# Second attention turns four heads behind its scores with seven buffers, and GpSimd waits for the normalisation before it splits weights

## The chip, the cores and the metric

The kernel runs on one core of one Trainium2 chip. The metric is the time of one execution in microseconds (us), measured on the device; runs of the same kernel give a median. One further execution was taken with the hardware profiler, and all rows below are from it.

## The reference, cut to what matters

Two layers of attention and feed-forward over 2048 tokens of width 256, float32, each of the four parts followed by a residual sum and a normalisation of the row:

```
x = layernorm(x + attention0(x))      # 16 heads, polynomial
x = layernorm(x + ffn0(x))            # dense, 1024 hidden
x = layernorm(x + attention1(x))      # 32 heads of 8 columns, softmax, in blocks of 256 tokens
x = layernorm(x + moe(x))             # shared expert + 2 of 8 experts

# attention1, for each of the 8 blocks of 256 tokens
scores = (q @ k.T) / sqrt(8) + rel_bias[None, None]
attn   = softmax(scores, axis=-1)
ctx    = attn @ v
out    = ctx @ wo.T
```

The change lies in attention1, in the loads and splits of the expert weights that run beside it, and in the first part of the mixture of experts, which uses those weights.

## The kernel before, in words

The program is written engine by engine: SyncE (SP) issues the loads and stores, TensorE (PE), ScalarE (ACT), VectorE (DVE) and GpSimd (POOL) each have one list of instructions, and semaphores hold them together. Every engine works its own list strictly in the order of the program. There are four phases: 0 and 1 (first attention and first feed-forward, interleaved), 2 (second attention, `phase2` on each engine), 3 (`moe`).

**Phase 2** makes eight iterations, one for each block of 256 tokens. In each, all engines step through the 32 heads with `for h in range(H2)`. The work of one head is a chain:

1. `scores` (PE): at every even h the scores of heads h and h+1, four matmuls, into one of three PSUM banks (`SCORE_BANKS`). It waits until `least` of head h-2 is done (`biased_ready`).
2. `least` (DVE): adds the bias, finds the row minimum of the negated scores, writes `prob(h)`, one of four SBUF buffers, and `mneg`. It waits for the scores, and until the turn of head h-4 has read the buffer.
3. `exponential` (ACT): exp of `prob(h)` in place, two instructions.
4. `turn` (PE): four transposes of `prob(h)` into one of two PSUM banks. At step h, head h-2 is turned. It waits for the exp of that head and until the head two before it has been taken out of its bank.
5. `take`: the turned head is copied to SBUF, by ACT for six heads of eight (`on_act`), by DVE for the other two. ACT takes head h-2 at its step h, ahead of exp(h); DVE takes head h-3 at its step h.
6. `mix` (PE): every fourth step, the product of four heads with V, sixteen matmuls.

Between these, at steps given by the tables `PE2`, `ACT2` and `DVE2`, lies all other work of the iteration: for the next block the transpose of x (`x_turn`), the projections (`qk`, `v`), their splits in a high and a low part (`hi_parts`, `lo_parts`), the transposes of the heads (`heads`, 8 transposes); for the block before, the division (`context`), its transposes (`c_turn`, `ct_turn`), the output projection (`project`), and on DVE the residual sum, the statistics (`add`) and the normalisation (`norm`). `x_turn` waits for the last copies of the heads (`heads_out`), because it uses the same bank.

**GpSimd in phase 2** splits weights of the mixture of experts in high and low parts: per iteration i the gate and up weights of expert i (`expert_part(i, 0)`), half a unit of the shared expert (`shared_part(i)`), and the down weights of expert i (`expert_part(i, 1)`, not in the last). `split` is one copy and one subtraction, both from the one raw buffer `wraw`; when it is done, SP may load the next piece (`raw_free`). After that GpSimd computes the reciprocal deviation for block i (`layernorm_rstd`), for which DVE's `norm` waits, and goes straight on to the split of the next expert.

**Phase 3** starts with 18 gate/up products of the shared expert on PE (`gate_up(n)`), with the router's choice on DVE between them (`choose`, `slots_in`). GpSimd first does constants, `layernorm_rstd` of the last block, and then the last three splits: the shared unit `SH_KEPT` (needed by `gate_up(4)`), half a unit (needed by `gate_up(5)`), and the down weights of expert 7. Then it scatters the tokens, for which it waits for `slots_ready`.

Of the kernel before, what the change touches and what calls it, by code (L numbers as in the profile page):

```python
# [30 lines left out]
P = 128  # L31
# [54 lines left out]
MIX_BANK = 4  # L86

# [4 lines left out]
def program(nc, x, rope, ln, aw0, wu1, aw2, rel, wu3, router, sel, out):  # L92
    with ExitStack() as ctx:
# [130 lines left out]
        mneg = small[:, 312:320]  # L224
# [159 lines left out]
        def dmas(load):  # L384

            e, kind = divmod(load - LOADS[2], 3)
            if load < LOADS[2]:
                return 1
            if load == LOADS3:
                return 4  # L390
            return 2 * len(list(pieces(e))) if kind == 0 and e < NEXP else 1
# [48 lines left out]
        def _(sp):  # L440
# [91 lines left out]
            def expert_weights(i):  # L532

                sp.wait_ge(raw_free, LOADS[2] + 3 * i + 1)
                for t, a, b, at in pieces(i):
# [4 lines left out]
                sp.wait_ge(raw_free, LOADS[2] + 3 * i + 2)  # L540
                half = slice(SH_HALF * (i % 2), SH_HALF * (i % 2 + 1))
                sp.dma_start(wraw[:, 0:SH_HALF], wu3[SH_FROM + i // 2, :, half]).then_inc(raw_ready, 16)
                if i == iterations[2] - 1:
                    return
# [27 lines left out]
            x3_rows(0, 4, rows_in)  # L572
            sp.wait_ge(raw_free, LOADS3)
            sp.dma_start(wraw[:], wu3[SH_FROM + SH_KEPT]).then_inc(raw_ready, 16)
            sp.wait_ge(raw_free, LOADS3 + 1)
            shared_last()
# [28 lines left out]
        def _(pe):  # L605
# [298 lines left out]
            def phase2():  # L904
# [21 lines left out]
                def turn(i, h, first):  # L926
# [4 lines left out]
                    for kt in range(2):  # L931
                        for t in range(2):
                            m = pe.transpose(ps[:, 2 + h % 2, S * kt + P * t:S * kt + P * (t + 1)],  # L933
                                             prob(h)[:, t, P * kt:P * (kt + 1)], ident[:])
# [76 lines left out]
            def moe():  # L1011
# [24 lines left out]
                def gate_up(n):  # L1036
# [150 lines left out]
            pe.wait_ge(split_w, PARTS3 - 1)  # L1187
# [4 lines left out]
        def _(act):  # L1192
# [227 lines left out]
            def phase2():  # L1420
                n = iterations[2]

                def exponential(i, h, first):

                    act.wait_ge(biased_ready, H2 * i + h + 1)
                    for t in range(2):
                        k = 2 * (h % 4) + t
                        m = act.activation(prob(h)[:, t, :], prob(h)[:, t, :], ACT.Exp, scale=-1.0,  # L1428
# [33 lines left out]
                take(n - 1, H2 - 1, False)  # L1462
# [116 lines left out]
        def _(dve):  # L1579
# [358 lines left out]
            def phase2():  # L1938
# [3 lines left out]
                def least(i, h, first):  # L1942

                    dve.wait_ge(score_ready[2], H2 * i + h + 1)
                    if h >= 4 or not first:

                        dve.wait_ge(probT_turned, H2 * i + h - 3)
                    apart(dve)
                    for t in range(2):
                        k = 2 * (h % 4) + t  # L1950
                        m = dve.tensor_tensor_reduce(prob(h)[:, t, :], ps[:, SCORE_BANKS[h % 3], S * t:S * (t + 1)],  # L1951
# [554 lines left out]
```

## Time and profile before

| | before |
|---|---|
| median of 3 runs | 1031.82 us (1025.96 to 1033.84) |
| profiled execution, own time | 1028.5 us |
| its span | 1026.6 us |
| PE busy | 888.6 us (87%) |
| DVE busy | 716.0 us (70%) |
| ACT busy | 682.8 us (67%) |
| POOL busy | 285.5 us (28%) |
| mean granted clock of TensorE | 0.965 |

Phase 2 lies between about 379 and 802 us of the span. Busy times are unions over the instructions of an engine in one execution; an engine that is not busy is waiting for another. PEclk is the share of full speed that TensorE's clock was granted: 1.00 is 2.4 GHz, 0.50 is 1.2 GHz.

### The profile page before, as it was taken

The numbers are of one execution on the slowest core, as the hardware profiler recorded it, in microseconds if no ns is written. First come the engines' busy times: TensorE is split into PE (matmuls) and PEld (weight loads), VectorE is DVE, ScalarE is ACT, GpSimd is POOL, SyncE is SP. The second block draws the span as 40 slices with busy tenths as digits, with TensorE's granted clock in tenths as the row PEclk, the third lists the DMA queues.
The fourth block names the chain that finished last, engine by engine and source line by source line (L and its number), as shares of the span: only waits on it lengthen the run. The fifth ranks groups of instructions, "written<-read, shape, count | busy, mean of one in ns | idle before, by whom it ended". The sixth has DMA issues, their size and how long they took to land.

```text
span 1026.6 us, 21001 instructions
## 1 busy us (share of the span) xinstructions
PE 888.6 (87%) x7200; PEld 715.4 (70%) x7200; DVE 716.0 (70%) x2092; ACT 682.8 (67%) x1475; POOL 285.5 (28%) x373
## 2 busy tenths in 40 slices
PE   4666899999899988898988898988888899799994
PEld 3455787788788985565666666666655788698884
DVE  6778877877865557788887877788877553265437
ACT  2675766857764349888888787888888323266644
POOL 1347632323432202002020202010101217434436
PEclk8888999999999999999999999999999999899997
DMA  6203022010000102011110101110011302244444
GB/s 186 62 2 104 1 74 83 12 32 22 12 31 22 42 11 64 2 26 39 26 40 26 40 25 40 26 31 24 22 32 50 98 15 101 83 109 115 114 131 163
DMA packets 58569, 54.87 MB, mean 53 GB/s; under 512 B 17921, under 2 KB 54017, under 8 KB 58466
## 3 DMA queue, kind: packets, MB, share of 16 engines
q1 hardware_dynamic: 55058, 44.18, 14.9%
q0 software_dynamic: 3408, 9.34, 2.7%
q8 instruction: 61, 1.00, 0.4%
q14 instruction: 42, 0.34, 0.1%
HBM read 32.85 MB, written 20.65 MB: 52 GB/s over the span
## 4 chain that ended last, share of the span: by engine, by line
PE 45%; DVE 21%; ACT 15%; issue 10%; POOL 5%; DMA 3%; SPq 1%; DVEq 0%; ACTq 0%; POOLq 0%
PE ps L434 8%; PE ps L435 7%; PE ps L436 7%; ACT G L1428 6%; PE ps L933 5%; DVE G L1951 4%; PE ps L648 4%; POOL xs L2404 3%; PE ps L950 3%; PE ps L921 3%; ACT G L1438 2%; DVE RT L1754 1%; PE ps L719 1%; PE ps L663 1%; PE ps L1115 1%
## 5 line engine op out<-in xcount | busy, mean ns | idle before, releaser
L1428 ACT ACTIVATE G<-G,small 128x256 f32<-128x256 f32 x512 | 232.2, 509 | 54.3 <-DVE small L1951 52.9
L1951 DVE CUSTOM_DVE_ANT_0 G<-ps,nb 128x256 f32<-128x256 f32 x512 | 191.2, 420 | 74.7 <-PE ps L921 74.4
L933 PE MATMUL ps<-ident,G 128*128 128x128 f32 x1024 | 161.1, 287 | 37.0 <-ACT G L1428 34.5
L933 PEld LDWEIGHTS ps<-ident,G 128*128 128x128 f32 x1024 | 111.2, 143 | 74.0 <-ACT G L1428 57.9
L434 PE MATMUL ps<-WU 128*128 128x256 f32 x384 | 117.1, 305 | 14.5 <-DVE WU L1768 5.0
L1438 ACT COPY G<-ps 128x512 f32<-128x512 f32 x192 | 111.4, 580 | 13.2 <-PE ps L933 13.2
L2311 POOL TENSOR_SCALAR_AFFINE_SELECT G<-G 128x256 f32<-128x256 f32 x128 | 76.4, 621 | 152.9 <-ACT G L1283 152.6
L435 PE MATMUL ps<-WU 128*128 128x256 f32 x384 | 108.3, 282 | 0.0
L436 PE MATMUL ps<-WU 128*128 128x256 f32 x384 | 108.2, 282 | 0.0
L2273 POOL TENSOR_SCALAR small<-small 128x2 f32<-128x2 f32 x16 | 6.6, 412 | 342.3 <-DVE small L1605 342.3
L434 PEld LDWEIGHTS ps<-WU 128*128 128x128 f32 x384 | 72.7, 189 | 22.5 <-DVE WU L1781 8.4
L648 PE MATMUL ps<-ident,RT 128*128 128x128 f32 x512 | 72.7, 289 | 17.3 <-DVE RT L1754 14.5
L648 PEld LDWEIGHTS ps<-ident,RT 128*128 128x128 f32 x512 | 60.1, 148 | 26.3 <-issue 17.0
L1283 ACT ACTIVATE G<-ps 128x768 f32<-128x768 f32 x64 | 52.3, 818 | 35.2 <-PE ps L702 30.3
L950 PE MATMUL ps<-G 128*32 128x256 f32 x1024 | 72.8, 404 | 0.8 <-ACT G L1438 0.8
L435 PEld LDWEIGHTS ps<-WU 128*128 128x128 f32 x384 | 73.0, 190 | 0.2
L436 PEld LDWEIGHTS ps<-WU 128*128 128x128 f32 x384 | 72.8, 190 | 0.0
L921 PE MATMUL ps<-RT 32*128 32x256 f32 x512 | 65.2, 332 | 6.2 <-DVE small L1951 3.8
L921 PEld LDWEIGHTS ps<-RT 32*128 32x128 f32 x512 | 38.9, 187 | 42.2 <-issue 29.9
L2439 POOL DMA_INDIRECT yy<-G x39 | 37.5, 962 | 65.9 <-ACT G L1522 65.9
L1202 ACT CAST RT<-ps 128x512 fp32r<-128x512 f32 x64 | 36.9, 577 | 27.0 <-PE ps L648 27.0
L1295 ACT ACTIVATE wu_rows<-ps 128x256 f32<-128x256 f32 x64 | 24.4, 382 | 45.6 <-PE ps L436 45.5
(245 smaller groups left out, 2230.7 us busy)
## 6 DMA issues: line engine op xcount, KB each, us to landing
xs<-G SPq DMA_DIRECT2D x8, 645.0 KB, 6.8
G<-xs SPq DMA_DIRECT2D x39, 128.0 KB
G<-in_x SPq DMA_DIRECT2D x16, 256.0 KB, 2.9
G<-x SPq DMA_DIRECT2D x16, 256.0 KB, 3.1
wu_rows<-yy SPq DMA_DIRECT2D x8, 512.0 KB, 7.4
x<-G SPq DMA_DIRECT2D x15, 256.0 KB, 3.0
wu_rows<-in_wu SPq DMA_DIRECT2D x8, 384.0 KB, 6.1
wraw<-in_wu SPq DMA_DIRECT2D x8, 256.0 KB, 2.9
```

The source lines that it names most:

```text
L434: pe.matmul(o, lh, rh, start=start, stop=False, skip_group_check=True)
L435: pe.matmul(o, lh, rl, start=False, stop=False, skip_group_check=True)
L436: return pe.matmul(o, ll, rh, start=False, stop=stop, skip_group_check=True)
L648: m = pe.transpose(ps[:, bank, S * g + P * t:S * g + P * (t + 1)], w[:, t, 2 * n + g, :], ident[:])
L921: m = pe.matmul(ps[:, SCORE_BANKS[n % 3], S * t:S * (t + 1)], QT[r, g, P * t:P * (t + 1)], KTT[r, g, :], start=True, stop=True, tile_posit ...
L933: m = pe.transpose(ps[:, 2 + h % 2, S * kt + P * t:S * kt + P * (t + 1)], prob(h)[:, t, P * kt:P * (kt + 1)], ident[:])
L950: m = pe.matmul(ps[32 * j:32 * j + 32, MIX_BANK, S * (quad % 2):S * (quad % 2 + 1)], vp[:, kt, at:at + 32], probT(h)[:, kt, :], start=kt = ...
L1283: act.square(U(p), ps[:, b:b + 2, 0:384]).then_inc(squared, 1)
L1428: m = act.activation(prob(h)[:, t, :], prob(h)[:, t, :], ACT.Exp, scale=-1.0, bias=mneg[:, k:k + 1])
L1438: act.copy(probT(h), halves(2 + h % 2)).then_inc(probT_act, 1)
L1951: m = dve.tensor_tensor_reduce(prob(h)[:, t, :], ps[:, SCORE_BANKS[h % 3], S * t:S * (t + 1)], nbv[:, t, :], 1.0, -FMIN, ALU.add, ALU.min, ...
L2311: m = pool.affine_select(out=u, in_=u, compare_op=ALU.is_ge, fill=0.0, base=0, pattern=[[0, 2], [1, P]], channel_multiplier=-1)
```

## The change

- `TURN_LAG = 4`: at PE's step h head h-4 is turned, not h-2. ACT takes head h-4 at its step h, DVE head h-5. The mix moves from steps with h % 4 == 3 to h % 4 == 1, so that it still follows the takes by the same distance. After the last step four heads are left to turn, not two.
- `PROBS = 7`: seven buffers for the probabilities instead of four. Three of them lie where the gate and up weights of expert 7 go (`late`), so these weights can only be placed when phase 2 is over. `mneg` becomes sixteen columns.
- The tables are shifted: the work between the heads comes one step later, some of it two steps.
- The gate and up weights of expert 7 are no longer loaded and split in iteration 7, but after the shared unit and the half unit in phase 3: four pieces instead of three there, two in iteration 7 become one.
- GpSimd, after each `layernorm_rstd` of phase 2, waits until DVE's `norm` is done (`xo_ready`) before it goes on to the next split; also after the last one, in phase 3.

```diff
-PE2 = dict(heads=(25, 29, 1, 3), x_turn=5, qk=(8, 14), c_turn=(6, 8, 10, 12), ct_turn=17, v=19,
-           project=21)
-ACT2 = dict(heads=(26, 30, 1, 4), place_v=5, x_hi=5, context_hi=18, hi_parts=(9, 15), stage_v=20)
-DVE2 = dict(heads=(26, 30, 1, 4), outputs=(12, 20, 28, 4), x_lo=7, context=(7, 9, 11, 13),
-            context_lo=19, add=23, norm=25, lo_parts=(11, 17))
+PE2 = dict(heads=(26, 30, 2, 4), x_turn=6, qk=(9, 15), c_turn=(8, 10, 12, 14), ct_turn=17, v=20,
+           project=22)
+ACT2 = dict(heads=(27, 31, 3, 5), place_v=7, x_hi=6, context_hi=18, hi_parts=(10, 16), stage_v=21)
+DVE2 = dict(heads=(27, 31, 3, 5), outputs=(14, 22, 30, 6), x_lo=8, context=(9, 11, 13, 15),
+            context_lo=19, add=24, norm=26, lo_parts=(12, 18))
+TURN_LAG = 4
+PROBS = 7
...
-        def prob(h):
-
-            return WORK[:, 512 * (h % 4):512 * (h % 4 + 1)].rearrange("p (t k) -> p t k", t=2)
+        def prob(n):
+
+            slot = n % PROBS
+            late = EX_AT + 2 * EX * (NEXP - 1) + 512 * (slot - 4)
+            buf = WORK[:, 512 * slot:512 * (slot + 1)] if slot < 4 else wu_rows[:, late:late + 512]
+            return buf.rearrange("p (t k) -> p t k", t=2)
...
-                        if h >= 2 or not first:
-                            turn(i, h - 2, first)
-                        if h % 4 == 3 and (h > 3 or not first):
-                            mix(i if h > 3 else i - 1, (h - 7) // 4 % 8, first)
+                        if h >= TURN_LAG or not first:
+                            turn(i, h - TURN_LAG, first)
+                        if h % 4 == 1 and (h >= 9 or not first):
+                            mix(i if h >= 9 else i - 1, (h - 9) // 4 % 8, first)
...
-                for h in (H2 - 2, H2 - 1):
+                for h in range(H2 - TURN_LAG, H2):
                     turn(n - 1, h, False)
+                    if h == H2 - 3:
+                        mix(n - 1, H2 // 4 - 2, False)
...
                     if n == SH_KEPT:
+                        pe.wait_ge(split_w, PARTS3 - 1)
+                    if n == SH_KEPT + 1:
                         pe.wait_ge(split_w, PARTS3)
-                    if n == SH_KEPT + 1:
-                        pe.wait_ge(split_w, PARTS3 + 1)
...
-                        if on_act(h - 2) and (h >= 2 or not first):
-                            take(i, h - 2, first)
+                        if on_act(h - TURN_LAG) and (h >= TURN_LAG or not first):
+                            take(i, h - TURN_LAG, first)
...
-                    if h >= 4 or not first:
-                        dve.wait_ge(probT_turned, H2 * i + h - 3)
+                    if h >= PROBS or not first:
+                        dve.wait_ge(probT_turned, H2 * i + h - PROBS + 1)
...
-                        if not on_act(h - 3) and (h >= 3 or not first):
-                            take(i, h - 3, first)
+                        if not on_act(h - TURN_LAG - 1) and (h > TURN_LAG or not first):
+                            take(i, h - TURN_LAG - 1, first)
...
             for i in range(iterations[2]):
-                expert_part(i, 0)
+                if i < iterations[2] - 1:
+                    expert_part(i, 0)
                 shared_part(i)
                 if i < iterations[2] - 1:
                     expert_part(i, 1)
                     layernorm_rstd(2, i, 2)
+                    pool.wait_ge(xo_ready, NORMS[2] + i + 1)
...
             layernorm_rstd(2, iterations[2] - 1, 2)
+            pool.wait_ge(xo_ready, NORMS[2] + iterations[2])

             pool.wait_ge(y_ready[2], iterations[2])
-            split(LOADS3 - 1, PARTS3 - 1, shared(SH_KEPT, 0, 0, UNIT), shared(SH_KEPT, 1, 0, UNIT), wraw[:])
-            split(LOADS3, PARTS3, shared(SH_KEPT + 1, 0, 0, HALF_UNIT), shared(SH_KEPT + 1, 1, 0, HALF_UNIT), wraw[:, 0:HALF_UNIT])
-            at = EX_AT + 2 * EX * (NEXP - 1) + EX_GU
-            split(LOADS3 + 1, PARTS3 + 1, WF[:, at:at + EX_DOWN], WF[:, at + EX:at + EX + EX_DOWN], wraw[:, 0:EX_DOWN])
+            split(LOADS3 - 2, PARTS3 - 2, shared(SH_KEPT, 0, 0, UNIT), shared(SH_KEPT, 1, 0, UNIT), wraw[:])
+            split(LOADS3 - 1, PARTS3 - 1, shared(SH_KEPT + 1, 0, 0, HALF_UNIT), shared(SH_KEPT + 1, 1, 0, HALF_UNIT),
+                  wraw[:, 0:HALF_UNIT])
+            expert_part(NEXP - 1, 0)
+            expert_part(NEXP - 1, 1)
```

## Rows read from the trace of the kernel before

**Rows 1.** Windows: busy us (x instructions) per engine, granted clock, DMA share, GB/s

```profile
467.36:519.33 51.97, 45.78 (x414) 32.82 (x414) 42.45 (x170) 44.62 (x104) 6.75 (x8) 1.00 0.12 32
...
572.66:627.31 54.65, 48.65 (x414) 34.91 (x414) 42.32 (x170) 44.80 (x104) 6.76 (x8) 0.94 0.11 31
```

**Rows 2.** Groups of instructions by line, from 467.36 to 519.33

```profile
L933 PE MATMUL ps<-ident,G 128*128 128x128 f32 x130 | 20.2, 284 | 4.1 <-ACT G L1428 4.0
...
L950 PE MATMUL ps<-G 128*32 128x256 f32 x128 | 8.6, 385 | 0.0
...
L648 PE MATMUL ps<-ident,RT 128*128 128x128 f32 x32 | 4.2, 274 | 0.0
...
L663 PE MATMUL ps<-ident,G 128*128 128x128 f32 x16 | 2.4, 272 | 0.0
...
L1616 DVE TENSOR_SCALAR G<-G,small 128x256 f32<-128x256 f32 x2 | 2.2, 1153 | 0.0
```

**Rows 3.** Waits from 467.36 to 519.33: us in total, times, longest us

```profile
ACT G L1428 <- DVE small L1951: 5.8, 7, 1.4
...
PE ps L613 <- ACT RT L1202: 1.4, 1, 1.4
ACT G L1438 <- PE ps L933: 1.4, 2, 0.9
```

**Rows 4.** Timeline of PE, 502 to 510: start us, us, instructions, idle before

```profile
502.30 0.47 PE L434 MATMUL ps<-AW,RT 128*128 128x512 f32 x1
...
503.76 0.60 PE L933 MATMUL ps<-ident,G 128*128 128x128 f32 x4
...
505.29 0.50 PE L921 MATMUL ps<-RT 32*128 32x256 f32 x4
505.73 1.09 PE L933 MATMUL ps<-ident,G 128*128 128x128 f32 x8
...
507.79 0.66 PE L933 MATMUL ps<-ident,G 128*128 128x128 f32 x4
509.07 0.66 PE L933 MATMUL ps<-ident,G 128*128 128x128 f32 x4 [0.63 <-ACT G L1428]
```

**Rows 5.** Timeline around a normalisation, three engines, and the last normalisation

```profile
521.11 2.22 DVE L1616 TENSOR_SCALAR G<-G,small 128x256 f32<-128x256 f32 x2
...
521.17 1.68 POOL L2257 TENSOR_TENSOR WU<-wraw,WU 128x704 fp32r<-128x704 f32 x1
...
526.77 0.66 PE L933 MATMUL ps<-ident,G 128*128 128x128 f32 x4 [1.10 <-ACT G L1428]
...
817.09 0.72 DVE L1616 TENSOR_SCALAR G<-G,small 128x256 f32<-128x256 f32 x2
```

**Rows 6.** Windows of 3.4 us around falls of the granted clock

```profile
576.70:580.10 3.40, 1.63 (x20) 0.72 (x8) 3.40 (x15) 2.72 (x7) 1.33 (x2) 0.97 0.20 58
...
593.90:597.30 3.40, 2.01 (x15) 1.71 (x16) 3.12 (x12) 2.78 (x7) 0.00 (x0) 0.95 0.03 9
597.30:600.70 3.40, 3.40 (x26) 1.76 (x25) 1.90 (x9) 3.40 (x8) 0.00 (x0) 0.55 0.67 179
```

**Rows 7.** Timeline of phase 3, POOL and PE, and the spread of line 1754

```profile
813.87 0.82 POOL L2252 CAST AW<-wraw 128x768 fp32r<-128x768 f32 x1
814.77 1.85 POOL L2257 TENSOR_TENSOR AW<-wraw,AW 128x768 fp32r<-128x768 f32 x1
820.49 0.61 POOL L2252 CAST AW<-wraw 128x512 fp32r<-128x512 f32 x1 [3.87 <-DMA wraw<-in_wu]
...
825.98 1.30 POOL L2257 TENSOR_TENSOR WU<-wraw,WU 128x512 fp32r<-128x512 f32 x1
844.87 1.24 POOL L2404 DMA_INDIRECT xs<-G,small  x1 [17.59 <-DVE small L2098]
...
825.75 0.48 PE L434 MATMUL ps<-RT,AW 128*128 128x512 f32 x1
...
L1754 DVE TENSOR_TENSOR RT<-G,RT x32: 676/686/2308, 28.3 to 285.8; 128x512 fp32r<-128x512 f32 x32
```

More of the change, by code:

```diff
@@ L223, in program @@
         hrs = small[:, 248:312]
-        mneg = small[:, 312:320]
+        mneg = small[:, 602:618]
         eps_col = small[:, 320:321]
@@ L388, in dmas @@
                 return 1
+            if load == LOADS3 - 1:
+                return 4
             if load == LOADS3:
-                return 4
-            return 2 * len(list(pieces(e))) if kind == 0 and e < NEXP else 1
+                return 2 * len(list(pieces(NEXP - 1)))
+            return 2 * len(list(pieces(e))) if kind == 0 and e < NEXP - 1 else 1
         def raw_count(load):
@@ L530, in _, with expert_up @@
             sp.sem_inc(stored[2], 16)
-            def expert_weights(i):
-                sp.wait_ge(raw_free, LOADS[2] + 3 * i + 1)
-                for t, a, b, at in pieces(i):
+            def expert_up(e):
+                for t, a, b, at in pieces(e):
                     src = wu3[t, :, 0:2 * KT * P].rearrange("p (m k c) -> p m k c", m=2, k=KT)
@@ L539, in expert_weights @@
                         sp.dma_start(dst[:, :, m, at:at + b - a], src[:, m, :, a:b]).then_inc(raw_ready, 16)
-                sp.wait_ge(raw_free, LOADS[2] + 3 * i + 2)
+            def expert_weights(i):
+                last = i == iterations[2] - 1
+                if not last:
+                    sp.wait_ge(raw_free, LOADS[2] + 3 * i + 1)
+                    expert_up(i)
+                sp.wait_ge(raw_free, LOADS[2] + 3 * i + (1 if last else 2))
                 half = slice(SH_HALF * (i % 2), SH_HALF * (i % 2 + 1))
                 sp.dma_start(wraw[:, 0:SH_HALF], wu3[SH_FROM + i // 2, :, half]).then_inc(raw_ready, 16)
-                if i == iterations[2] - 1:
+                if last:
                     return
@@ L572, in _ @@
             x3_rows(0, 4, rows_in)
+            sp.wait_ge(raw_free, LOADS3 - 1)
+            sp.dma_start(wraw[:], wu3[SH_FROM + SH_KEPT]).then_inc(raw_ready, 16)
             sp.wait_ge(raw_free, LOADS3)
-            sp.dma_start(wraw[:], wu3[SH_FROM + SH_KEPT]).then_inc(raw_ready, 16)
+            shared_last()
             sp.wait_ge(raw_free, LOADS3 + 1)
-            shared_last()
+            expert_up(NEXP - 1)
             sp.wait_ge(raw_free, LOADS3 + 2)
@@ L933, in turn @@
                             m = pe.transpose(ps[:, 2 + h % 2, S * kt + P * t:S * kt + P * (t + 1)],
-                                             prob(h)[:, t, P * kt:P * (kt + 1)], ident[:])
+                                             prob(H2 * i + h)[:, t, P * kt:P * (kt + 1)], ident[:])
                     m.then_inc(probT_turned, 1)
@@ L1186, in _ @@
             phase2()
-            pe.wait_ge(split_w, PARTS3 - 1)
+            pe.wait_ge(split_w, PARTS3 - 2)
             moe()
@@ L1426, in exponential @@
                     for t in range(2):
-                        k = 2 * (h % 4) + t
-                        m = act.activation(prob(h)[:, t, :], prob(h)[:, t, :], ACT.Exp, scale=-1.0,
+                        k = 2 * (h % 8) + t
+                        p = prob(H2 * i + h)[:, t, :]
+                        m = act.activation(p, p, ACT.Exp, scale=-1.0,
                                            bias=mneg[:, k:k + 1])
@@ L1461, in phase2 @@
                 passes(n, one)
-                take(n - 1, H2 - 1, False)
+                for h in range(H2 - TURN_LAG, H2):
+                    if on_act(h):
+                        take(n - 1, h, False)
             def moe():
@@ L1944, in least @@
                     dve.wait_ge(score_ready[2], H2 * i + h + 1)
-                    if h >= 4 or not first:
-                        dve.wait_ge(probT_turned, H2 * i + h - 3)
+                    if h >= PROBS or not first:
+                        dve.wait_ge(probT_turned, H2 * i + h - PROBS + 1)
                     apart(dve)
                     for t in range(2):
-                        k = 2 * (h % 4) + t
-                        m = dve.tensor_tensor_reduce(prob(h)[:, t, :], ps[:, SCORE_BANKS[h % 3], S * t:S * (t + 1)],
+                        k = 2 * (h % 8) + t
+                        m = dve.tensor_tensor_reduce(prob(H2 * i + h)[:, t, :], ps[:, SCORE_BANKS[h % 3], S * t:S * (t + 1)],
                                                      nbv[:, t, :], 1.0, -FMIN, ALU.add, ALU.min, mneg[:, k:k + 1])
@@ L2354, in expert_part @@
                 at, n = EX_AT + 2 * EX * e + EX_GU * k, EX_DOWN if k else EX_GU
-                load = 3 * e + 2 * k
+                load = 3 * e + (2 * k if e < NEXP - 1 else k + 3)
                 split(LOADS[2] + load, PARTS[2] + load, WF[:, at:at + n], WF[:, at + EX:at + EX + n], wraw[:, 0:n])
@@ L2359, in shared_part @@
                 at = SH_HALF * i
-                split(LOADS[2] + 3 * i + 1, PARTS[2] + 3 * i + 1, WF[:, at:at + SH_HALF],
+                load = 3 * i + (1 if i < NEXP - 1 else 0)
+                split(LOADS[2] + load, PARTS[2] + load, WF[:, at:at + SH_HALF],
                       WF[:, at + SH_KEPT * UNIT:at + SH_KEPT * UNIT + SH_HALF], wraw[:, 0:SH_HALF])
             for i in range(iterations[2]):
-                expert_part(i, 0)
+                if i < iterations[2] - 1:
+                    expert_part(i, 0)
                 shared_part(i)
```

## The prediction

> **What bounds the kernel now.** I read the page first (which engine is busy), then the busy times of equal stretches of phase 2, then the waits and groups of one such stretch, then the timelines around two of its gaps, and last the granted clock.
>
> Phase 2 takes 423 us (379 to 802) in eight like iterations. An undisturbed one takes 51.97 us, in which TensorE is busy 45.8 us, ScalarE 44.6 and VectorE 42.5 [rows 1]. So no engine is the bound: three engines at 82 to 88% hold each other up. TensorE stands idle 6.2 us per iteration. Most of that is transposes waiting for the exponential, 4.0 us, and one wait of 1.4 us at `x_turn` (line 613), which needs ScalarE's last copy of the heads (line 1202) [rows 2, 3].
>
> Why it waits is seen in the loop of one pair of heads. The scores of a pair start at 505.29; the even head's transposes start at 507.79, 2.50 us later, and the odd head's at 509.07, 3.78 us later, after 0.63 us of idle time [rows 4]: minimum, exponential, a copy and a second exponential lie between. The odd head is turned one step after the next pair's scores, behind 0.44 of scores and 0.55 of the even turn. So a pair cannot follow its forerunner in less than 3.78 - 0.99 = 2.8 us, however little TensorE has to do in it. Pairs with much inserted work take longer, and the light ones give nothing back.
>
> The second gap comes once per iteration behind the normalisation. Line 1616's two instructions took 2.22 us while GpSimd's subtraction ran from 521.17; the last normalisation, with GpSimd at rest, took 0.72 [rows 5]. VectorE thus reaches the next minimum 1.5 us late, and TensorE then idles, 1.10 us at 526.77 [rows 5] and 0.45 shortly before.
>
> The third loss is the clock. Seven times in phase 2 it drops to 1.2 GHz for about 3.4 us, always right behind one of these two gaps: the stretch before had 1.63 us (behind the normalisation) or 2.01 us (at `x_turn`) of work in 3.4 [rows 6]. Four stand behind `x_turn`, three behind the normalisation. An iteration with two of them takes 54.65 instead of 51.97 [rows 1], so one costs 1.34 us.
>
> **The change part by part.** *Lag of four.* A head is now turned two pairs after its scores, so the exponential has 2.8 us per pair twice over; 2.50 and 3.78 us fit in. What remains is the bank: `turn(h)` needs the copy of head h-2, which ScalarE makes after the exponential of head h+1. That is 3.78 + 0.5 - 0.44 = 3.84 us per **two** pairs for even heads (the 0.5 is a copy and its signal, an estimate from the 1.28 between the two turns less one exponential). TensorE's least work in two pairs is 1.54 + 2.6 = 4.1 (below). So no loop forces a floor any more; the lists can average over about two pairs.
>
> To price this I add up TensorE's work per pair. Scores and two turns: 0.44 + 1.09 = 1.5 [rows 4]. A mix 1.07 (8.6 over 8), `heads` 1.05 (4.2 over 4), a `c_turn`, `ct_turn` or `x_turn` 0.6 (2.4 over 4) [rows 2]; `qk` 1.46, from 502.30 to 503.76 [rows 4], and `v` and `project` the same, since they have twice as many matmuls of half the columns. Before, by its tables, in order of the sixteen pairs: 2.55, 3.55, 2.1, 3.1, 3.55, 3.1, 2.1, 3.95, 2.1, 3.95, 2.95, 2.5, 2.55, 2.5, 2.55, 2.5; together 45.6, which is the 45.8 busy. Each raised to at least 2.8 they give 49.4, and with the gap at `x_turn` (1.4) and the one behind the normalisation (1.55) 52.3: the measured 51.97. The working holds, so I use it for the new tables: 2.5, 2.55, 3.55, 2.1, 4.55, 2.1, 3.1, 3.55, 3.1, 1.5, 3.95, 2.95, 2.5, 2.55, 2.5, 2.55, again 45.6. Bounds: if TensorE never waits 45.8; if every pair still takes the slower of TensorE's work and ScalarE's (2.56 with two copies, plus its inserted work), 49.8. With averaging over two pairs against ScalarE's mean 2.8 per pair (44.6 over 16 [rows 1]) it is 48.3. ScalarE's work is less than 2.8 in many pairs, so I take the middle of the two ends, **47.8, a gain of 4.2** (2.1 to 6.2).
>
> *x_turn.* It stays one step behind the last copy of the heads, but more TensorE work now lies between scores(4, 5) and it: 0.44 + 0.55 + 1.05 + 0.55 + 1.07 + 0.44 + 0.55 = 4.65. The chain to be awaited is 3.78 + 0.47 = 4.25. The 1.4 us go; this is within the 4.2.
>
> *Waiting for the normalisation.* VectorE's two instructions fall from 2.22 to about 0.72, seven times (within the 4.2 too). GpSimd starts its split some 1.1 us later. Behind it are queued only splits and, through `raw_free`, SP's loads of weights, the store of x3 and the load of the residual rows; nobody needs these for some 20 steps. Cover gone, they cost at most 1.1.
>
> *Seven buffers.* The minimum of head h needs the turn of head h-7, three steps back in TensorE's own list, ahead of the scores it waits for anyway: nothing. Position in memory: nothing.
>
> *First and last iteration* have less inserted work, thus less unevenness to gain: 2.5 each, an estimate, between 0 and the full amount. **Sum for the iterations:** 6 x 4.2 + 2 x 2.5 = 30 (ends 17 and 50).
>
> *Clock.* Both gaps that stood before every drop shrink. All seven: 9.4 us; none: 0. I take five, 6.7.
>
> *Drain.* Four heads are left instead of two. TensorE's list has the same work in the same order but for two turns and a mix that come after the transposes of x3, where it idled anyway: 0 to 1, I take 0.5.
>
> *Phase 3.* After the last block GpSimd now waits for the normalisation, which ends at 817.81, before it splits the shared unit, which started at 813.87: 3.9 later. It is then done at about 820.6; `gate_up(4)` starts at 825.75 [rows 5, 7]: hidden, 5 us to spare. The half unit has landed 3.87 later and is split by 826.5; its user is 6.5 behind `gate_up(4)`. Then the added piece: 3.9 for landing, about 2.5 for its split (1.68 for the subtraction [rows 5] and half as much for the copy), and the down weights 2.8 + 2.0: ready at about 838, where it was 827.3. The scatter starts at 844.87 [rows 7], the experts later: hidden, 7 to spare. But these splits now run beside VectorE's choice of experts, whose chain ends in that scatter. An instruction with both inputs in SBUF normally takes 0.69, once 2.31 (line 1754 [rows 7]), so one collision can cost 1.6: 0 to 1.9, I take 0.5. The Trainium skill ("SBUF — State Buffer", Who interferes with whom) states that such an instruction locks out a GpSimd one that reads SBUF, and the second to come blocks for the whole of the first. By it the collision is certain if they overlap and costs up to one subtraction, 1.3; the spread of line 1754 agrees.
>
> **Sum.** Profiled execution: 1028.5 - 30 - 6.7 + 0.5 + 0.5 = 992. It was itself 3.3 below the median of the three runs, so from the median the same sum gives 995.
>
> **The rivals.**
> *A. Copies become the bound (slower).* ScalarE's copy of head h-4 stands ahead of exp(h) in its list. If TensorE is busy with an inserted block (ten per iteration, 1.05 to 1.46 each), ScalarE blocks on the copy while the exponentials it could do are ready, and TensorE later waits for the bank. Today this wait (line 1438) is 1.4 us per iteration [rows 3]. It decides if it rises by more than the 4.2 gained, to 5.6, that is 0.4 us at each of the ten blocks. At 0.55 each, iterations become 1.3 longer, the clock drops stay: 1031.8 + 10 = 1042. For: both engines are near 86% busy. Against: the copies stand in the same place relative to the turns as before.
> *B. Only the normalisation helps.* If the minimum to exponential wait (5.8 us on ScalarE [rows 3]), which the lag doesn't touch, is what sets the pace, the lag gives little: 7 x 1.5 = 10 and the three drops behind the normalisation, 4: 1018. This is also the case where the lag does not do what it says.
> *C. TensorE never waits.* 50 + 9.4 gone: 972.
> *D. The collision of phase 3 eats part:* at most 2 us, inside the range.
>
> **How the numbers follow.** Chances: the forecast (980 to 1012) 0.66, C or near it 0.08, B 0.17, A 0.06, some stall that I don't see, about no change, 0.03. Faster by over 1% means under 1021.5 (about 1% is what runs of this kernel can tell, since they spread by 0.8%). B lies partly above that: faster 0.85, within 1% 0.09, slower 0.06. The range 979 to 1015 reaches from near C to the better half of B; the low end of the iterations' sum with two drops saved is 1031.8 - 17 - 2.7 + 2 = 1014.
>
> **What would show it.** Right: iterations of 47 to 49 us with the clock at 1.00; line 933's wait for ScalarE under 1.5 us per iteration; no wait at line 613; line 1616 at 0.36 each; at most three drops of the clock in phase 2. TensorE should show 93 to 96% busy there. In phase 3 the shared unit's split about 4 us later with no wait of `gate_up(4)`. Wrong: iterations above 50 us with waits moved to line 1438 (A), or ScalarE still waiting 5 us per iteration for line 1951 (B).

## The result and the profile after

| | before | changed |
|---|---|---|
| median of 6 runs each | 1029.77 us (1025.85 to 1034.16) | 1013.98 us (1012.62 to 1018.19) |
| ratio, 95% interval | | 0.9837 (0.9801 to 0.9874) |
| profiled execution, its span | 1028.5, 1026.6 | 1012.62, 1010.4 |

The change makes the kernel 1.6% faster, 16 us. I forecast 36 us, with 979 to 1015 as the range: right in sign, the median just inside the range's edge, and more than twice too much in size.

The page of the changed kernel, busy time per engine:

```profile
PE 876.8 (87%) x7200; PEld 714.4 (71%) x7200; DVE 704.7 (70%) x2092; ACT 680.1 (67%) x1475; POOL 284.0 (28%) x373
```

VectorE lost 11.3 us of busy time (716.0 to 704.7), most of it in seven normalisations at 1.5 us. The shares are what they were, so nothing can be read from the page about the lag. The windows of the changed kernel tell more. Each runs from one reciprocal deviation on GpSimd to the next, as in [rows 1], but the last, which runs to the scatter; columns as there:

```profile
470.20:520.81 50.61, 44.99 (x417) 33.05 (x416) 40.65 (x170) 44.40 (x104) 6.80 (x9) 1.00 0.13 33
520.81:571.15 50.34, 44.42 (x411) 32.43 (x410) 40.59 (x170) 44.40 (x104) 6.79 (x8) 1.00 0.12 34
571.15:623.00 51.85, 46.22 (x414) 34.30 (x413) 40.56 (x170) 44.52 (x104) 6.80 (x8) 0.97 0.11 32
...
725.25:770.80 45.55, 39.77 (x386) 28.80 (x385) 37.36 (x161) 41.15 (x94) 6.80 (x8) 1.00 0.13 39
770.80:829.42 58.62, 52.47 (x376) 44.24 (x376) 34.92 (x99) 23.99 (x47) 14.75 (x27) 1.00 0.21 63
```

An iteration with the clock at 1.00 takes 50.4 us, where it took 51.97 [rows 1] and I wanted 47.8. TensorE is busy 44.4 of it and still waits 5.9 us, against 6.2 before. (Its work is the same, and yet its busy time fell from 45.8 to between 44.4 and 44.7. The profile models the ends of matmuls, so the line between busy and waiting is blurred by 1 us and more per iteration; the length of the window is not.) The waits of the second window show for what:

```profile
DVE G L1972 <- PE ps L937: 5.4, 5, 2.3
...
DVE wu_rows L1972 <- PE ps L937: 3.2, 3, 1.6
ACT wu_rows L1447 <- DVE small L1972: 2.7, 4, 1.2
ACT G L1447 <- DVE small L1972: 2.6, 3, 1.6
PE ps L949 <- DVE G L1982: 2.5, 3, 1.3
...
PE ps L937 <- DVE small L1972: 1.3, 2, 1.0
...
PE ps L664 <- ACT RT L1220: 0.9, 1, 0.9
```

(Lines 937, 949, 1447 and 1972 are 921, 933, 1428 and 1951 of before: scores, turn, exponential and minimum; 1982 is VectorE's copy of a turned head, 1961 before. A buffer of the probabilities is now called G or wu_rows.) The 4.0 us in which transposes waited for the exponential and the 1.4 at `x_turn` [rows 2, 3] are gone, as forecast. In their place turns wait 2.5 us for **VectorE's** copy, which holds the PSUM bank, scores wait 1.3 for the minimum, and `heads` waits 0.9. ScalarE waits for the minimum as much as before, 5.3 us against 5.8.

The 16 us by stretches of the two profiles: up to the start of phase 2's first iteration 1.0 us more; from there to the first deviation 1.8 **more** (87.13 against 85.29); the next five iterations 11.5 less (255.05 against 266.59), of which the clock 3.8 (two falls of the granted clock, "drops" from here on, of 1.4 us each instead of five of 1.34); the last iteration 5.0 less (45.55 against 50.53), of which the clock 1.3; up to the scatter 1.8 less (58.62 against 60.39), of which the clock 1.3; the tail 0.7 less.

The normalisation does what was forecast: `L1637` now has a median of 0.41 us and a longest of 0.49, where one took up to 1.9. GpSimd waits 0.95 us for it, as the timeline of the changed kernel has it at the split behind one of them:

```profile
573.13 0.77 POOL L2273 CAST WU<-wraw 128x704 fp32r<-128x704 f32 x1 [0.95 <-DVE G L1637]
```

### The profile page after: what moved, and what is told of

Read it like the earlier page. It is cut to its first block, busy times and chain, and to the rows that moved or that the text cites. A ratio compares the mean times of both kernels' runs of the same rounds, so it can differ in the third digit from the quotient of the medians.

```text
span 1010.4 us, 21008 instructions
## 1 busy us (share of the span) xinstructions
PE 876.8 (87%) x7200; PEld 714.4 (71%) x7200; DVE 704.7 (70%) x2092; ACT 680.1 (67%) x1475; POOL 284.0 (28%) x373
## 4 chain that ended last, share of the span: by engine, by line
PE 48%; DVE 18%; ACT 15%; issue 9%; POOL 5%; DMA 3%; SPq 0%; DVEq 0%; ACTq 0%; POOLq 0%
PE ps L442 9%; PE ps L443 8%; PE ps L444 8%; PE ps L949 5%; PE ps L966 5%; ACT G L1447 4%; PE ps L664 3%; POOL xs L2430 3%; PE ps L937 3%; ACT wu_rows L1447 3%; ACT G L1457 2%; DVE G L1972 2%; PE ps L735 1%; DVE RT L1775 1%; PE ps L1133 1%
## 5 line engine op out<-in xcount | busy, mean ns | idle before, releaser
L1447 ACT ACTIVATE G<-G,small 128x256 f32<-128x256 f32 x296 | 133.3, 511 | 25.2 <-DVE small L1972 25.0
L1972 DVE CUSTOM_DVE_ANT_0 G<-ps,nb 128x256 f32<-128x256 f32 x296 | 111.1, 420 | 44.3 <-PE ps L937 43.9
L1457 ACT COPY G<-ps 128x512 f32<-128x512 f32 x192 | 112.1, 584 | 11.8 <-PE ps L949 11.3
L1447 ACT ACTIVATE wu_rows<-wu_rows,small 128x256 f32<-128x256 f32 x216 | 97.6, 510 | 15.4 <-DVE small L1972 15.2
L949 PE MATMUL ps<-ident,G 128*128 128x128 f32 x592 | 91.5, 282 | 13.5 <-DVE G L1982 9.6
L1972 DVE CUSTOM_DVE_ANT_0 wu_rows<-ps,nb 128x256 f32<-128x256 f32 x216 | 81.3, 420 | 29.8 <-PE ps L937 29.4
L949 PEld LDWEIGHTS ps<-ident,G 128*128 128x128 f32 x592 | 65.4, 142 | 27.0 <-issue 8.4
L1301 ACT ACTIVATE G<-ps 128x768 f32<-128x768 f32 x64 | 52.3, 817 | 35.5 <-PE ps L718 30.6
L949 PE MATMUL ps<-ident,wu_rows 128*128 128x128 f32 x432 | 66.8, 282 | 10.2 <-DVE G L1982 8.9
L966 PE MATMUL ps<-G 128*32 128x256 f32 x1024 | 68.5, 385 | 5.1 <-ACT G L1234 4.4
```

The lines of the kernel that those rows point to most:

```text
L966: m = pe.matmul(ps[32 * j:32 * j + 32, MIX_BANK, S * (quad % 2):S * (quad % 2 + 1)], vp[:, kt, at:at + 32], probT(h)[:, kt, :], start=kt = ...
L1301: act.square(U(p), ps[:, b:b + 2, 0:384]).then_inc(squared, 1)
L1447: m = act.activation(p, p, ACT.Exp, scale=-1.0, bias=mneg[:, k:k + 1])
L1457: act.copy(probT(h), halves(2 + h % 2)).then_inc(probT_act, 1)
L1972: m = dve.tensor_tensor_reduce(prob(H2 * i + h)[:, t, :], ps[:, SCORE_BANKS[h % 3], S * t:S * (t + 1)], nbv[:, t, :], 1.0, -FMIN, ALU.add, ...
```

## The experiments

Iteration times are windows from one deviation to the next with the granted clock at 1.00, unless said otherwise. Totals are compared by their ratio to the kernel before, run on the same chip.

**e1, the wait alone.**

```diff
                     layernorm_rstd(2, i, 2)
+                    pool.wait_ge(xo_ready, NORMS[2] + i + 1)
```

> The kernel before with one edit: GpSimd waits for the normalisation in the seven iterations of phase 2. The whole change took 16 us off. Theory 1 (the two parts of the change bring separate gains, the lag most of it): line 1616 falls from 1.11 to 0.36 us, an undisturbed iteration from 52.0 to 50.5 or more, and the drops of the clock behind the normalisation go: 6 to 12 us faster than before. Theory 2 (the normalisation gap was the only thing that set the pace, the lag gives nothing): nearly all of the 16 us, undisturbed iterations at 50.5 as in the changed kernel. Theory 3 (VectorE's lost 1.5 us is absorbed elsewhere): within 3 us of before.

Ratio 0.9896 (0.9835 to 0.9956): 1018.76 us against 1027.77, 9 us of the 16. Theory 1's numbers fit, but not its words: it is the wait, not the lag, that brings most.

**e2, the lag alone**, is the changed kernel without this line and its like in phase 3.

```diff
                     layernorm_rstd(2, i, 2)
-                    pool.wait_ge(xo_ready, NORMS[2] + i + 1)
...
             layernorm_rstd(2, iterations[2] - 1, 2)
-            pool.wait_ge(xo_ready, NORMS[2] + iterations[2])
```

> The changed kernel without GpSimd's waits for the normalisation. Theory 1: 4 to 10 us faster than before, iterations at about 51; line 613 no longer waits. Theory 2 (the lag gives nothing): no faster than before, 1028 to 1032. Theory 3 (the lag alone does it, the normalisation's 1.5 us vanish in the deeper pipeline): 1014, the same as the changed kernel.

Ratio 1.0004 (0.9974 to 1.0034): 1029.01 against 1027.77. Without the wait the lag gives nothing, which is theory 2 for this run; yet e1 leaves 0.6% to the lag once the wait is there (the intervals of e1 and of the change overlap), so the parts don't simply add. A window of e1, then one of e2:

```profile
470.55:521.12 50.57, 45.77 (x414) 32.77 (x414) 41.05 (x170) 44.58 (x104) 6.83 (x9) 1.00 0.13 33
...
726.01:774.53 48.52, 42.67 (x388) 30.06 (x388) 37.36 (x161) 41.52 (x94) 6.83 (x8) 0.96 0.11 29
```

```profile
523.71:575.77 52.06, 44.42 (x411) 32.40 (x410) 42.31 (x170) 44.45 (x104) 6.76 (x8) 1.00 0.11 32
...
735.57:782.88 47.31, 39.79 (x386) 28.79 (x385) 39.11 (x161) 41.20 (x94) 6.77 (x9) 1.00 0.12 38
```

In a full iteration the wait is worth 1.4 us (51.97 to 50.57) or, with the lag, 1.7 (52.06 to 50.34); the lag -0.1 without it and 0.2 with it. Only in the last iteration (the second window of each), where nothing of a next block stands between the heads, does the lag pay: with the wait from 47.2 (48.52 less a drop's 1.34) to 45.55, without it from 49.2 to 47.31. The rest of the lag's gain with the wait is the clock: past 400 us e1 has five drops in phase 2, the changed kernel two.

Why the lag alone gives nothing stands in e2's trace, VectorE and TensorE around a normalisation:

```profile
524.93 2.45 DVE L1637 TENSOR_SCALAR G<-G,small 128x256 f32<-128x256 f32 x2
527.29 0.68 DVE L1982 COPY G<-ps 128x512 f32<-128x512 f32 x1
...
528.12 1.07 PE L949 MATMUL ps<-ident,wu_rows 128*128 128x128 f32 x8 [2.55 <-DVE G L1982]
```

The normalisation of step 26 stands right ahead of VectorE's copy of step 27. TensorE can't turn the next head into that bank and idles 2.55 us. The exponential of that head was done by 523.2; the bank is not free.

**e3, the copy ahead of the inserted work.**

```diff
-                        if not on_act(h - TURN_LAG - 1) and (h > TURN_LAG or not first):
-                            take(i, h - TURN_LAG - 1, first)
                         least(i, h, first)
+                        if not on_act(h - TURN_LAG) and (h >= TURN_LAG or not first):
+                            take(i, h - TURN_LAG, first)
```

> The changed kernel with VectorE copying the turned head h-4 right behind the minimum of head h, ahead of the work that is inserted in that step, instead of head h-5 at the head of the next step (the same copy, earlier by the inserted work of 0.6 to 1.4 us in eight steps of an iteration). Theory 1 (what is left of TensorE's idle time is the bank that VectorE's late copy holds, 2.5 us per iteration): the waits of line 949 for line 1982 go, iterations fall from 50.4 by 1 to 2 us, 8 to 15 us faster than the changed kernel. Theory 2 (ScalarE's wait for the minimum, 5.3 us per iteration, sets the pace whatever TensorE does): within 3 us of the changed kernel, or slower, since minimums come later.

Ratio 0.9780 (0.9730 to 0.9830), 1006.96 us, against 0.9837 of the change: another 6 us, though the intervals overlap. The waits for line 1982 are all but gone (0.2 of 2.5), but an iteration falls by only 0.5. Its window, and two of TensorE's waits in it:

```profile
522.25:572.07 49.82, 45.05 (x411) 32.43 (x410) 40.62 (x170) 44.35 (x104) 6.83 (x9) 1.00 0.12 34
```

```profile
PE ps L937 <- DVE small L1972: 1.2, 2, 0.9
...
PE ps L949 <- DVE G L1982: 0.2, 1, 0.2
```

The rest, some 3 us, is the clock: no drop between 400 and 860 us, where the changed kernel has two. Those two, at 611.9 and 714.3, come 0.2 to 0.4 us behind the longest wait for VectorE's copy, the one that e3 takes away:

```profile
611.66 0.85 PE L949 MATMUL ps<-ident,wu_rows 128*128 128x128 f32 x4 [1.32 <-DVE G L1982]
...
713.92 0.72 PE L949 MATMUL ps<-ident,wu_rows 128*128 128x128 f32 x4 [1.32 <-DVE G L1982]
```

Theory 1 is right about the wait and wrong about what it is worth: of 2.3 us taken away, 1.8 come back elsewhere, 1.2 as other waits of TensorE and 0.6 as busy time.

**e4, five buffers.**

```diff
-PROBS = 7
+PROBS = 5
```

> The changed kernel with five buffers for the probabilities instead of seven. The minimum of head h then needs the turn of head h-5, which for odd h stands behind the scores of h in TensorE's list by two turns. Theory 1 (the buffers only have to reach past the scores; the last two are never the late one): within 3 us of the changed kernel. Theory 2 (VectorE runs ahead into the spare buffers and this evens the load out): 5 to 15 us slower, with VectorE waiting for line 949.

Ratio 0.9876 (0.9822 to 0.9929); its iteration of 50.34 us is that of seven buffers to the last digit. The last two buffers buy nothing that can be measured. The fifth still lies where the weights of expert 7 go, so whether they had to move at all (four buffers) wasn't tried.

**e5 and e6, other places.** e5 is the changed kernel with

```diff
-..., qk=(9, 15), ... v=20,
+..., qk=(10, 15), ... v=19,
-... hi_parts=(10, 16), stage_v=21)
+... hi_parts=(11, 16), stage_v=20)
-... lo_parts=(12, 18))
+... lo_parts=(12, 17))
```

> The changed kernel with other steps for five pieces of work, so that TensorE's and VectorE's heavy pairs lie less on each other's light ones (qk 10 and 15, hi_parts 11 and 16, lo_parts 12 and 17, v 19, stage_v 20). If each pair of heads costs the largest of the three engines' work in it, the changed tables sum to 52.9 us per iteration and these to 49.6, against 52.3 for the kernel before and 50.9 for it with the wait alone (measured 52.0 and 50.6). Theory 1 (the lag evens out little, and the change's tables took back what it gained): iterations fall from 50.4 by 1 to 3 us, 8 to 20 us faster than the changed kernel. Theory 2 (where the work stands inside the iteration hardly matters once heads are turned four late): within 3 us.

e6 has e3's edit as well.

> The tables of the run before and VectorE's copy right behind the minimum. Theory 1 (two separate losses): the copy brings about 7 us as it did alone, on top of what the tables bring; iterations of 48 to 49. Theory 2 (one and the same loss, VectorE's late copy behind inserted work): no better than the better of the two alone.

Ratios 0.9776 (0.9746 to 0.9806) and 0.9772 (0.9742 to 0.9802), iterations of 50.05 and 49.93. The tables bring 0.3 us per iteration, not 3.3; together with the copy nothing more than the copy alone. For the iterations that is theory 2. The gain of e5 in the total, 6 us against the changed kernel, is more than the 3 that theory 2 allowed, and again mostly drops of the clock that don't happen (one between 400 and 800 us).

**e7, the same idea with a lag of two.**

```diff
-... qk=(8, 14), ... ct_turn=17, v=19,
+... qk=(8, 13), ... ct_turn=18, v=17,
-... context_hi=18, hi_parts=(9, 15), stage_v=20)
+... context_hi=19, hi_parts=(9, 14), stage_v=18)
-... context_lo=19, ... lo_parts=(11, 17))
+... context_lo=20, ... lo_parts=(11, 16))
```

(on top of e1)

> The kernel before with the wait of GpSimd and tables that put TensorE's heavy pieces into pairs without a mix (qk 8 and 13, v 17, and what follows them); lag two, four buffers. The sum of the pairs' largest work is 49.9 against 50.9. Theory 1 (the placing of the work is worth as much as the lag): iterations of 49.5 to 50, 5 to 8 us faster than the run with the wait alone, as fast as the changed kernel. Theory 2 (only the lag can lower the floor of a light pair, 2.8 us): within 2 us of the run with the wait alone.

Ratio 0.9987 (0.9961 to 1.0013), iterations of 52.4:

```profile
525.39:577.83 52.44, 45.91 (x415) 32.73 (x413) 41.09 (x170) 44.75 (x104) 6.80 (x8) 1.00 0.12 32
```

Both theories missed: it is 1.8 us per iteration **slower** than e1, where the sums said 1.0 faster. In this window TensorE waits for the exponential again, 4.7 us against 3.2 in e1's:

```profile
PE ps L933 <- ACT G L1428: 4.7, 11, 1.4
```

This falsifies the counting by pairs itself, with two engines or with three: it hit the kernel before by luck. It says that with a lag of two an iteration is sensitive to where the work stands. With four, e5's move was worth 0.3, but those of e9 and e13 below 1.1 and 1.2, so the deeper lag doesn't take that away.

**e8, four copies from VectorE to ScalarE.**

```diff
-ACT_TAKES_EVEN = (0, 4)
+ACT_TAKES_EVEN = (0, 2, 4)
```

> The changed kernel with ScalarE copying seven of eight turned heads instead of six: four copies per iteration (0.47 us each, 1.9 in all) go from VectorE to ScalarE. Theory 1 (VectorE's lateness holds the bank): half of the waits of line 949 for line 1982 go, 1 to 5 us faster than the changed kernel. Theory 2 (ScalarE's load sets the pace): iterations 1 to 2 us longer, 8 to 15 us slower than the changed kernel. Both at once would come out within 2 us.

Ratio 0.9859 (0.9830 to 0.9887), iterations of 50.63, 0.2 more than the changed kernel: theory 2's direction, an eighth of its size. The waits for VectorE's copy fell only from 2.5 to 2.1 us, not by half as theory 1 had it.

**e10 and e11, a small instruction added for each head.** In the changed kernel, behind the minimum and behind the exponential:

```diff
                     m.then_inc(biased_ready, 1)
+                    dve.tensor_copy(small[:, 618 + h % 8:619 + h % 8], nb[:, 0:1])
```

```diff
                     m.then_inc(prob_ready, 1)
+                    act.copy(small[:, 626 + h % 8:627 + h % 8], nb[:, 0:1])
```

> The changed kernel with one more instruction of one column on VectorE behind each minimum (some 0.06 to 0.1 us, 32 per iteration, so 2 to 3 us of VectorE's time). VectorE is busy 40.6 us of 50.4. Theory 1 (VectorE's list holds up the others): most of the added time is seen in the iteration, 1.5 to 3 us, 12 to 24 us in the total. Theory 2 (VectorE has slack in its 8 us of waiting for scores): under a third of it, below 8 us in the total.

> The changed kernel with one more instruction of one column on ScalarE behind each exponential (some 0.1 to 0.2 us, 32 per iteration, so 3 to 6 us of ScalarE's time). ScalarE is busy 44.4 us of 50.4. Theory 1 (VectorE sets the pace and ScalarE waits 5.3 us for it): under half of the added time is seen. Theory 2 (ScalarE sets the pace): all of it or more, 24 to 48 us in the total.

On the chip of these runs the kernel before took 1051 us (the scatters of phase 3 were slower there), so only ratios and iterations count: 0.9872 (0.9836 to 0.9909) and 0.9979 (0.9929 to 1.0030). A window of each:

```profile
526.28:577.28 51.00, 44.94 (x415) 32.70 (x413) 42.61 (x202) 44.70 (x104) 6.80 (x8) 1.00 0.12 33
```

```profile
690.81:742.01 51.20, 44.81 (x414) 32.70 (x413) 40.59 (x170) 47.12 (x136) 6.80 (x9) 1.00 0.10 28
```

Against 50.4 to 50.6 of the changed kernel, VectorE: 2.0 us more busy, about 0.5 us longer. ScalarE: 2.7 more busy, about 0.8 longer. **A quarter to 0.3 us per microsecond added, on either engine.** That is theory 2 of e10 and theory 1 of e11 by their bounds: neither engine is the bound, and neither has slack. e11's total lost more, since the clock fell seven times between 400 and 700 us, about 1.6 us each (54.36 us in a window with two, 51.20 in one with none).

**e9 and e13, taking away single waits.** e9 is e3 with

```diff
-PE2 = dict(heads=(26, 30, 2, 4), x_turn=6, qk=(9, 15), ... v=20, ...
+PE2 = dict(heads=(26, 30, 2, 5), x_turn=7, qk=(10, 16), ... v=21, ...
-ACT2 = dict(heads=(27, 31, 3, 5), place_v=7, x_hi=6, ... hi_parts=(10, 16), stage_v=21)
+ACT2 = dict(heads=(27, 31, 3, 6), place_v=6, x_hi=7, ... hi_parts=(11, 17), stage_v=22)
-DVE2 = dict(heads=(27, 31, 3, 5), ... x_lo=8, ... lo_parts=(12, 18))
+DVE2 = dict(heads=(27, 31, 3, 6), ... x_lo=9, ... lo_parts=(13, 19))
```

> The changed kernel with VectorE's copy right behind the minimum, and the places moved at which TensorE still waited in that run: the fourth heads a step later (5, x_turn 7), V placed a step earlier (6), qk 10 and 16, v 21 and what follows them. TensorE's idle time in an iteration of that run was 0.97 us at heads for ScalarE's copy, 0.71 at the first mix for V, 0.61 at v for the low parts, 1.2 at scores for the minimum, 1.2 at turns and others; 4.7 in all of 49.8. Theory 1 (these waits are each their own): 1.5 to 2.3 us per iteration, iterations of 47.5 to 48.3, 10 to 18 us faster than the run with the copy alone. Theory 2 (ScalarE and VectorE are behind on the whole, and the wait taken away at one place turns up at the next): under 0.8 us per iteration, within 6 us.

Ratio 0.9719 (0.9661 to 0.9777), on the chip of e10 and e11, the best of all; its interval lies below the change's. Iteration:

```profile
520.20:568.91 48.71, 44.38 (x411) 32.56 (x410) 40.76 (x170) 44.21 (x104) 6.81 (x8) 1.00 0.12 35
```

Half of the 2.3 us taken away, 1.1, stayed away, between the bounds of the two theories. The other half came back, above all in one place, `x_turn`:

```profile
539.52 0.66 PE L629 MATMUL ps<-ident,G 128*128 128x128 f32 x4 [1.43 <-ACT RT L1220]
```

Each of e9's three drops between 400 and 800 us comes 1.2 to 1.5 us behind the start of these transposes.

e13 puts that one later (x_turn 8, x_hi 8, x_lo 10, qk 11 and 16, hi_parts 12 and 17, lo_parts 14 and 19).

> The tables of the spread run with x_turn one step later (8, x_hi 8, x_lo 10, qk 11, hi_parts 12, lo_parts 14), since TensorE still waited 1.43 us there for ScalarE's copy of the heads. Spread run: iterations of 48.7. Theory 1 (single waits, each its own): 47.3 to 47.9. Theory 2 (the wait turns up again at the next place): 48.3 to 49.0, and a wait of 0.7 us or more of TensorE that was not there.

Ratio 0.9754 (0.9698 to 0.9810), which can't be told from e9's, but iterations of 49.93, 1.2 us longer than e9's. The 1.43 is gone and in its place are, in TensorE's timeline,

```profile
546.24 0.50 PE L442 MATMUL ps<-AW,RT 128*128 128x512 f32 x1 [0.43 <-DVE RT L1642]
...
554.80 0.50 PE L442 MATMUL ps<-AW,RT 128*128 128x512 f32 x1 [1.09 <-DVE RT L1665]
```

The projections now wait for VectorE's low parts, which had less time left. So far this is theory 2: a wait taken away turns up at the next place. It doesn't explain why e13 is longer, though: TensorE's waits in an iteration add up to 4.1 us in e13 and 4.2 in e9, and the difference stands in its busy time for the same work (44.38 against 45.48):

```profile
571.50:621.43 49.93, 45.48 (x414) 32.88 (x413) 40.60 (x170) 44.15 (x104) 6.82 (x8) 1.00 0.12 34
```

Those 1.2 us are not located.

**e12, the early copy without GpSimd's waits.** e3 with the two lines of e2 left out.

> The changed kernel with VectorE's copy right behind the minimum and without GpSimd's waits for the normalisation. With the late copy, leaving the waits out cost 1.7 us per undisturbed iteration (52.1 against 50.4), since the slow normalisation of step 26 stands right ahead of the copy of step 27 and TensorE's next turn needs the bank. Theory 1 (the bank is the road on which the normalisation's 1.5 us reach TensorE): with the copy ahead of the normalisation the waits are worth under 0.7 us per iteration, iterations of 49.9 to 50.5. Theory 2 (they reach it by the late minimum and exponential as well): 51.2 to 51.6, 9 to 13 us slower than the run with the copy and the waits.

Ratio 0.9843 (0.9784 to 0.9902). Iterations:

```profile
577.08:628.30 51.22, 45.30 (x414) 32.72 (x413) 42.04 (x170) 44.28 (x104) 6.76 (x8) 1.00 0.12 33
```

1.4 us more than with the waits (49.82). My theory 1 falls: the bank was the road of the 1.5 us in e2, but with that road shut they come by the minimum: scores wait 2.3 us for it in this window, against 1.2 in e3's, and ScalarE 5.9 against 4.8.

```profile
ACT wu_rows L1447 <- DVE small L1972: 3.5, 2, 1.9
...
ACT G L1447 <- DVE small L1972: 2.4, 4, 0.8
PE ps L937 <- DVE small L1972: 2.3, 2, 1.5
```

In all three pairs (before and e1, e2 and the change, e12 and e3) the normalisation's delay of 1.5 us costs 1.4 to 1.7, that is in full, while e10's 2.0 us, spread over 32 heads, cost 0.5.

## Why the prediction was wrong in size

**What bounds the kernel, the gaps and their order:** right. The three kinds of loss were the ones named, and the gap behind the normalisation is worth what it was priced at, 1.4 to 1.7 us per iteration (e1).

**The lag of four: the step that failed.** It is most of the 20 us that are missing: 25 were forecast for the six full iterations together, and at 1.6 each they brought some 10. "So no loop forces a floor any more; the lists can average over about two pairs", and from it 47.8 us and a gain of 4.2 per iteration. Measured: 50.4; of the 1.6 gained the wait brings 1.4 and the lag 0.2. The loop over the exponential did open, as worked out: in the changed kernel's window no matmul of a turn waits for it. What I did not price is the other loop of the same turn. I took the copy that frees the bank to be ScalarE's, 0.5 us behind an exponential. A quarter of the copies are VectorE's, they stand behind whatever work is inserted in VectorE's list, and turns waited 2.5 us per iteration for them. VectorE was left out of the sum of pairs altogether, though it too was busy 42.5 us of 52. e3 takes just these waits away, and 1.8 of 2.3 us return elsewhere; e13's rows show a part of such a return; e10 and e11 give both engines a slope of 0.25 to 0.3. So it isn't one forgotten term. What fits all of this, but is argued and not shown: three engines of about equal load pass their work on with one or two places of room, two banks for turned heads and three for scores, which the change leaves as they were, and a longer lag adds room only between the exponential and the turn. The price had a second fault. Its upper end, "if TensorE never waits 45.8", took TensorE's busy time for fixed, and the same work showed 44.4 to 45.8 in these runs.

**The counting by pairs** was a wrong instrument. It gave 52.3 for 51.97, which I took for proof. The sum over three engines did so too (52.3, and 50.9 for e1's 50.6), but gave 52.9 for the changed kernel's 50.4, and then missed e7 by 2.5 us (49.9 for 52.4) and the step from the changed kernel to e5 by 3 (3.3 for 0.3).

**First and last iteration,** 2.5 each: the last gained 3.6 at equal clock, of which by e1 the wait 2.0 and the lag 1.6. The first lost 1.8, which no step had: at its start the clock now falls to 1.2 GHz for 6.8 us. With a lag of four TensorE has no turns to make for the first four heads. In the stretch ahead of the fall it was busy 2.00 us of 3.40, in the same stretch of the kernel before 2.81; that the missing turns are the cause is inferred. The kernel before, then three windows of the changed kernel:

```profile
379.80:383.20 3.40, 2.81 (x23) 2.09 (x22) 3.25 (x18) 2.66 (x6) 0.94 (x2) 1.00 0.00 0
```

```profile
379.80:383.20 3.40, 2.00 (x16) 1.42 (x16) 2.60 (x13) 1.70 (x4) 0.13 (x1) 1.00 0.00 0
...
383.90:387.30 3.40, 3.03 (x14) 2.40 (x15) 3.13 (x15) 3.32 (x8) 0.19 (x1) 0.50 0.01 2
387.30:390.70 3.40, 3.08 (x16) 2.28 (x14) 1.68 (x6) 1.86 (x5) 0.00 (x0) 0.59 0.48 151
```

All twelve profiles with a lag of four have this drop, starting between 382 and 387 us; the three with a lag of two (before, e1, e7) do not.

**Clock,** 6.7 forecast: five of the seven drops went, as I took it; with the new long one some 5 us net remain. The drops were tied to the two gaps rightly, but the two that stay stand behind a third one, the wait for VectorE's copy (e3), which the prediction didn't have.

**Waiting for the normalisation, seven buffers, drain:** no cost is seen, as said; e4 shows that the sixth and seventh buffer give nothing.

**Phase 3.** Hidden as forecast: the shared unit's split is done at 804.30, `gate_up(4)` starts at 809.41 without a wait; the last split ends at 821.41, GpSimd then waits 8 us for the slots. The collision was taken at 0.5 (0 to 1.9) and is there, 0.9 us in VectorE's chain to the scatter. VectorE's comparison beside GpSimd's subtraction, and the same instruction again without it:

```profile
820.37 1.18 DVE L2075 TENSOR_TENSOR G<-G 128x128 f32<-128x128 f32 x1
...
823.02 0.29 DVE L2075 TENSOR_TENSOR G<-G 128x128 f32<-128x128 f32 x1
```

```profile
820.12 1.29 POOL L2278 TENSOR_TENSOR WU<-wraw,WU 128x512 fp32r<-128x512 f32 x1
```

It ends 0.14 us after the subtraction does (821.55 and 821.41). The Trainium skill ("SBUF — State Buffer", Who interferes with whom) says that the second to come blocks until the first is done; these rows agree: the comparison, the later to start, isn't done before the subtraction is.

**The rivals.** Rival B ("only the normalisation helps", 17% against the forecast's 66%) came true in the iterations: the normalisation brought 1.4 us and the lag 0.2, and the sign of being wrong that the prediction named for it came with it, iterations above 50 us and ScalarE's wait for the minimum (5.8 us [rows 3]) still at 5.3. Its reason, that this wait sets the pace, isn't shown: e10's 2.0 us more on VectorE cost 0.5. The measured median, 1014, stands between its 1018 and the forecast. That it fell inside the range is owed to the range's width, whose upper edge was put where B's better half lies, and not to the price of the lag. Rival A did not come: the copies of ScalarE wait 0.9 us, less than the 1.4 of before.

What stays open: which of the loops (the two banks of the turned heads, the three of the scores, the order in VectorE's list) gives back the time that a removed wait had cost. More PSUM banks would tell, but all eight are in use, and that was not tried.

## What to carry to other kernels

When three engines that feed each other are each at 82 to 88%, a gap on one of them is a symptom: check for every buffer of the handover (here the banks, not only the SBUF buffers) who frees it and what stands ahead of that instruction in its list, before granting a deeper pipeline more than a fraction of the idle time. A wait that is one lump, like a normalisation slowed by GpSimd's copies beside it, cost its full length here even in the deeper pipeline, so take lumps away first. And a model that reproduces one measured number is not tested; use it on a second kernel before it prices a change.

## What the runs showed of the hardware

That the clock can fall where a deeper lag starts: in the first iteration the granted clock stood at 1.2 GHz for 6.8 us in all twelve profiles with a lag of four, and the first iteration of the changed kernel came out 1.8 us longer. That small shifts decide over drops elsewhere: with iterations of 49.8 to 51.2 us, the changed kernel has two such drops later in phase 2, e3 none and e11 seven, at 1.3 to 1.6 us each, which is as much of a total's difference as the edits themselves. Those of the changed kernel and of e9 each stand right behind a wait of TensorE of 1.3 to 1.4 us. And that VectorE's `tensor_tensor` with both inputs in SBUF took 1.18 us instead of 0.29 beside a subtraction of GpSimd.
